# Output stores moved from SyncE's queue, mostly at the end, to ScalarE's own queue, one 192 KB group in each step

## The reference

```python
h = jnp.maximum(_layernorm(x), 0.0)
agg = jax.ops.segment_sum(edge_attr, dst, num_segments=12500)
t = jnp.concatenate([h, agg], axis=-1)
t = jax.nn.relu(t @ W1 + b1)
t = jax.nn.relu(t @ W2 + b2)
t = t @ W3 + b3
out = x + ((t - mean(t)) * rsqrt(var(t) + 1e-5) * ln_w + ln_b)
```

## Time and profile before

| | us |
|---|---|
| median of 3 runs (321.7 to 322.6) | 322.18 |
| the profiled execution, its own time | 321.9 |
| its span, first to last instruction | 320.1 |
| PE busy (matmuls) | 274.8 (86%) |
| VectorE busy | 246.4 (77%) |
| GpSimd busy | 178.5 (56%) |
| ScalarE busy | 149.7 (47%) |
| moved by DMA | 116.48 MB, mean 364 GB/s |

### The profile page before, as it was taken

How to read it: one execution, slowest core, us unless ns; L and a number is a source line. 1 busy time by engine, 2 the same in 40 slices (tenths; PEclk the granted TensorE clock), 3 DMA queues, 4 the chain that set the end, 5 groups by cost and what they waited for, 6 DMA issues and landing times. The chain is left out here.

```text
span 320.1 us, 12312 instructions
## 1 busy us (share of the span) xinstructions
PE 274.8 (86%) x3927; PEld 186.4 (58%) x3927; DVE 246.4 (77%) x944; ACT 149.7 (47%) x407; POOL 178.5 (56%) x208
## 2 busy tenths in 40 slices
PE   2959998998979887898888888899888888899881
PEld 0736665666646655566556666566555656566550
DVE  4944588888758887777787887778787887878785
ACT  1442555555415545545444545554444545554622
POOL 8634555566546565455565665555556565555511
PEclk9976999999979999999999999999999999999997
DMA  7999999999999999999999999999999999999992
GB/s 227 354 373 374 373 373 374 373 390 373 389 373 382 380 374 389 373 373 373 373 373 373 373 373 374 373 374 373 373 373 373 373 373 373 373 373 373 383 385 80
DMA packets 79454, 116.48 MB, mean 364 GB/s; under 512 B 3312, under 2 KB 79440, under 8 KB 79440
## 3 DMA queue, kind: packets, MB, share of 16 engines
q1 hardware_dynamic: 78426, 115.85, 102.5%
q10 hardware_dynamic: 1014, 0.46, 0.5%
HBM read 109.90 MB, written 6.40 MB: 363 GB/s over the span
## 5 line engine op out<-in xcount | busy, mean ns | idle before, releaser
L777 POOL TENSOR_SCALAR place<-iota,rows_at 128x128 f32<-128x128 f32 x131 | 104.5, 801 | 107.1 <-PE place_ps L426 98.4
L415 PE MATMUL part_ps<-ring,onehot 128*32 128x128 f32 x3120 | 115.1, 282 | 25.9 <-DMA ring<-in_edge_attr 24.9
L415 PEld LDWEIGHTS part_ps<-ring,onehot 128*32 128x32 f32 x3120 | 79.4, 111 | 72.4 <-issue 51.9
L931 DVE TENSOR_TENSOR agg<-place_ps,agg 128x128 f32 x131 | 38.0, 290 | 53.7 <-PE place_ps L426 51.9
L426 PE MATMUL place_ps<-place,part 128*128 128x128 f32 (+1 forms) x262 | 64.9, 330 | 2.7 <-POOL place L777 2.3
L785 POOL TENSOR_TENSOR xs<-xs,vecs 128x384 f32 (+2 forms) x33 | 54.8, 1659 | 19.0 <-ACT h L646 19.0
L855 DVE TENSOR_TENSOR onehot<-iota,local_t 128x768 f32<-128x768 f32 x66 | 63.5, 964 | 0.3 <-issue 0.3
L632 ACT ACTIVATE part<-part_ps 128x128 f32<-128x128 f32 x131 | 34.9, 267 | 48.5 <-PE part_ps L415 46.8
L426 PEld LDWEIGHTS place_ps<-place,part 128*128 128x128 f32 (+1 forms) x262 | 40.0, 192 | 30.0 <-issue 22.6
L646 ACT ACTIVATE h<-xs,x_shift,x_rstd 128x128 f32 (+2 forms) x98 | 41.3, 483 | 2.4 <-DVE x_shift L848 2.4
L662 ACT ACTIVATE hid<-hid_ps,b1s 128x384 f32<-128x384 f32 (+1 forms) x33 | 19.0, 576 | 47.5 <-PE hid_ps L450 47.5
(11 more groups left out here) (86 smaller groups left out, 202.0 us busy)
## 6 DMA issues: line engine op xcount, KB each, us to landing
ring<-in_edge_attr SPq DMA_DIRECT2D x130, 768.0 KB, 11.6
xs<-in_x SPq DMA_DIRECT2D x32, 192.0 KB, 10.1
out_x<-xs SPq DMA_DIRECT2D x15, 384.0 KB
dst_i<-in_dst SPq DMA_DIRECT2D x1, 768.0 KB
ring<-in_edge_attr SPq DMA_DIRECT2D x1, 192.0 KB, 10.1
out_x<-xs SPq DMA_DIRECT2D x1, 192.0 KB
out_x<-xs ACTq DMA_DIRECT2D x1, 192.0 KB
xs<-in_x SPq DMA_DIRECT2D x1, 96.0 KB
```

What stands on the lines that cost most here:

```text
L415: last = nc.tensor.matmul(part_ps[par_q % 2][s * WIN:(s + 1) * WIN, 0:D], onehot[:, oct_par, first + s, j, :], e[:, s, j * D:(j + 1) * D], ...
L777: nc.gpsimd.tensor_scalar(place[:, par_q % 2, :], iota[:, 0:P], rows_at[:, k:k + 1], None, ALU.is_equal).then_inc(place_ready, 1)
L931: nc.vector.tensor_tensor(v, place_ps[par_q % 2][:, 0:P], v, ALU.add).then_inc(added, 1)
```

## The change

SP loads only, until the end. ACT issues one group's store (192 KB) at the end of each of its steps 3 to 29, for group i-3 (groups 0 to 26), after a wait on `out_ready`. SP stores groups 27 to 30 singly behind the tail load, and the last, short one. Nothing else is changed.

```diff
-STORED_EARLY = 8
+BEHIND = 3
...
-                def store_two(g):
-                    sp.wait_ge(out_ready, g + 2)
-                    sp.dma_start(out[bass.ds(g * CHUNK, 2 * CHUNK), :].rearrange("(g p j) f -> p g (j f)", p=P, j=PER),
-                                 xs[:, bass.ds(g * CHUNK, 2 * CHUNK)].rearrange("p (g e) -> p g e", g=2)).then_inc(stored, 16)
...
                     step(0, 0, 0)
-                    with sp.Fori(0, STORED_EARLY // 2) as t:
-                        step(2 * t + 1, 1, t)
-                        step(2 * t + 2, 0, t + 1)
-                        store_two(2 * t)
-                    with sp.Fori(STORED_EARLY // 2, (STEPS - 3) // 2) as t:
+                    with sp.Fori(0, (STEPS - 3) // 2) as t:
                         step(2 * t + 1, 1, t)
                         step(2 * t + 2, 0, t + 1)
...
-                    for g in range(STORED_EARLY, GROUPS - 2, 2):
-                        store_two(g)
-                    store(GROUPS - 2)
+                    by_act = STEPS - 1 - BEHIND
+                    for g in range(by_act, GROUPS - 1):
+                        store(g)
                     store_last(GROUPS)
...
-                    def step(i, first=False, more_x=False):
+                    def store_behind(g):
+                        act.wait_ge(out_ready, g + 1)
+                        act.dma_start(group_rows(out, g), xg(g)).then_inc(stored, 16)
+
+                    def step(i, first=False, more_x=False, storing=True):
...
                         copy_ht(i + 1)
+                        if storing:
+                            store_behind(i - BEHIND)
...
-                    step(0, first=True)
-                    with act.Fori(1, STEPS - 2) as i:
+                    step(0, first=True, storing=False)
+                    for i in range(1, BEHIND):
+                        step(i, storing=False)
+                    with act.Fori(BEHIND, STEPS - 2) as i:
                         step(i)
```

More of the change, by code:

```diff
@@ L337, in fast @@
                                  edges[TAIL0:EDGES, :].rearrange("(p j) f -> p (j f)", j=PER)).then_inc(edges_loaded[tail], 16)
-                    for g in range(STORED_EARLY, GROUPS - 2, 2):
-                        store_two(g)
-                    store(GROUPS - 2)
+                    by_act = STEPS - 1 - BEHIND
+                    for g in range(by_act, GROUPS - 1):
+                        store(g)
                     store_last(GROUPS)
-                    sp.wait_ge(stored, 16 * ((GROUPS - 2) // 2 + 2 + len(LAST_PARTS)))
+                    sp.wait_ge(stored, 16 * (GROUPS + len(LAST_PARTS)))
                 def general():
```

## The result

The changed kernel takes 329.32 us (median of 4 runs, 328.86 to 330.86) against 321.94 us for the kernel before on the same chip (321.15 to 322.60): ratio 1.025, 95% interval 1.0221 to 1.0278, so 7.4 us slower. The profiled span is 327.0 us against 320.1.

What follows compares the result with a forecast made beforehand. The prediction took the edge loads, at 373 GB/s, to bound the kernel. Single stores +7.6, pairs no longer issued -2.8 and compute catching up -0.3 gave +4.5 us: 326.7 us against the median, range 321.7 to 332.

Steps and rivals of the forecast that it cites:

- The bound: Kernel body: edge loads at 373 GB/s set the 8.96 us step; stores issued among outstanding loads are paid in time.
- The price of a pair: Two groups stored together among the loads on SP's queue delay them by 0.71 us; four such stores, 2.8 us.
- The price of a single store on ACT's queue: One group's store among the loads, issued by ACT, delays them by 0.28 us; 27 of them, 7.6 us.
- the lift: Time around a store with the DMA rate above the loads' 373 GB/s; windows near 398 predicted for 3 to 4 us.
- The signs: Profile after: about 380 GB/s, steps of 9.2 us, windows near 398 for 3 to 4 us, last edge load near 296.5.
- The compute catching up: Behind the last full quad: PE's 1.8 us lag shrinks when loads come slower, -0.3 us.
- ACT and SP: Issuing engines: ACT's store issue, 0.66 us at most, fits its 1.18 us idle behind `copy_ht`; SP gains nothing.
- The end: Behind the last load: groups 27 to 30 are stored beside compute as before; the shorter queue gives nothing.
- Full price: Rival: stores among loads give little or nothing back, 0.46 to 0.53 us each; 331.5 to 333.3 us; chance 0.14.
- Free stores: Rival: stores among loads cost the loads nothing, about -2.5 us, 319.7; chance 0.17 for free or nearly free.
- ACT held: Rival: ACT's store issue takes up to 2.77 us, overrunning 0.55 us per step, 15 us, about 337; chance 0.07.

## Why the prediction was right, and where its size was off

**The bound.** Right: the body runs at the rate of the loads, and stores among them are paid in step length (8.96 to 9.38 us), not in any engine's work.

**The price of a pair.** Right: 0.71 us, read from the lifted rate, was 0.72 by the step length over six pairs of the run that stored 13 in a row. What was read in it, that one engine at a store lifts the rate, did not hold as it stands: in the us behind ACT's store the loads alone ran at 399 GB/s.

**The price of a single store on ACT's queue.** This is the term that was mis-sized. I took 0.28 us, on the ground that ACT's weight loads had also landed late, so that its stores would be taken up at different times by the DMA engines. It measured 0.42 us. The stores do wait, 3.8 us from issue (229.16) to the first packet (232.9), but then they are taken up everywhere at once: the 16 completion signals come within 0.3 us in the median, and the lift is under 2 us. A late landing was no evidence of a spread one. 27 x 0.14 us are 3.8 us too little. What I took for ACT's queue is what holds on SP's: there it measured 0.26 us.

That the change still came out within the stated +2.3 to +7.7 us is in part luck: 0.42 lies outside the 0.2 to 0.4 us per store that this band stands for, and with the other terms as put it would have been +8.2 us. The compute caught up 1.4 us more than was put. The signs had told it: the lift was under 2 us and not 3 to 4, the step 9.38 us and not 9.2, the last full quad issued at 298.6 and not near 296.5.

The Trainium skill, page "DMA: Bandwidth & Descriptors", section "Issuing engines are not separate DMA queues", says that DMAs of all issuing engines interleave on the same 16 DMA engines, and that another issuer saves only the sequencer's time. The runs agree that nothing is gained by ACT's queue; they add that the issuer isn't indifferent: the same stores cost 0.42 us on ACT's queue and 0.26 on SP's. The same page, section "Queues, rings and completion order", has each DMA engine take turns between queues at the granularity of a packet. The trace agrees, as far as shares of time can tell, once the store has begun: from 233 to 234 us the two queues have 54.0% and 52.2% of the engines' time. It doesn't explain the 3.8 us before that, which no run here does.

**The compute catching up.** I put 0.3 us; it was 1.7 us: 0.7 up to the last quad's sum and 1.0 behind it, where VectorE's add had been 1.2 us late before. The two errors, +3.8 and -1.4 us, leave 2.4 us; the spans of the two profiled executions differ by 6.9 us, the forecast was 4.5.

**ACT and SP.** Right: the issue took 0.36 us, ACT still waited 1.3 us for PE behind it, and an eighth of the bytes took all but 0.04 us per step of the loss away. Nothing gained by SP's shorter list of issues is seen.

**The end.** Right that it gave nothing: from 313 to 314 us the DMA engines move nothing at all, and from 320 to 321 again, before the last stores at 323.9.

**The rivals.** Full price was the nearest to what happened: its condition, all engines starting together, held, and so did its lower case, packets that alternate with loads and last 1 us. Its price for that, 0.46 us, is close to 0.42; the lift of the us behind makes up the difference. My chance of 0.14 for it was too low beside 0.62 for the other. Free stores: nothing of it. In quarters on SP's queue, the form nearest to it, a group still cost 0.17 us. ACT held: no. Of the range, the ends 321.7 and 332 are a little wide for their own prices: 0.11 us gives 321.8 by the execution's own time, 0.47 us 331.8 against the median.

## What to carry to other kernels

In a kernel bound by its loads, a store costs what it takes from the loads, so ask first where no load is outstanding: behind the last load, beside the closing compute, 22 groups were written here for nothing; with 30 the last stores had to wait behind them. Where stores must go among loads, small pieces on the same queue, one behind each load, cost 0.17 us per 0.197 MB, whole groups 0.26, pairs 0.36, and a queue of their own 0.42. Where the loads never pause, a profile's GB/s in windows of 1 us gives that price directly: (bytes of the store - bytes moved above the loads' own rate) / the loads' rate.

## What the runs showed of the hardware that was not expected

- Over 140 us of the body loads alone ran at 373 GB/s, with stores among or behind them windows show up to 406: the DMA engines could do more than the loads alone drew from them. In the us behind an ACT store the loads alone reached 399.
- The same store, from the same rows, cost the loads 0.42 us when ScalarE issued it and 0.26 us when SyncE did. On SyncE's queue the rate stays lifted for 4 to 5 us per store and its 16 completion signals are 3.6 us apart; on ScalarE's it is under 2 us (a pair: under 3) and 0.3 us.
- A store on ScalarE's otherwise empty queue had its first packet 3.8 us after its issue, and so did each of the changed kernel's 27 stores among the loads (3.8 to 3.9). The store of group 31, with the DMA engines idle, began 0.9 us after its issue (323.50 to 324.36). Why it waits so much longer while the loads run, and is then taken up everywhere at once, no run here tells.
